# One fixed matmul order for every attention period, and batch 1's second-norm transposes inside the last h1 product

## What is computed

```python
x = x + attn(layernorm(x))     # causal, 16 heads of 64; q, k, v and output projections
x = x + xattn(layernorm(x))    # one head of 256 onto 64 context rows per batch, masked by columns
x = x + ffn(layernorm(x))      # w3 gelu(h2 gelu(h1 (silu(w1 x) * (w2 x)))), ternary weights, scaled
```

## Time and profile before

| | |
|---|---|
| median of 3 runs | 1447.77 us (1446.35 to 1448.05) |
| profiled execution | 1446.44 us, of which the span from the first to the last instruction is 1444.7 us |
| mean granted TensorE clock over the span | 0.997 |
| busy share of the span | PE 99%, PEld 85%, DVE 84%, ACT 70%, POOL 42% |
| the chain that ended last | PE 90%, DVE 5%, ACT 3%, issue 1%, POOL 1% |
| DMA | 113.54 MB, mean 79 GB/s |

### The profile page before, as it was taken

One profiled execution on the slowest core, in us unless ns is written; L12 is line 12 of the kernel. 1 busy time (PEld: TensorE's weight loads), 2 busy tenths in 40 slices (PEclk: granted clock), 3 DMA queues, 4 the chain that ended last, 5 costly groups with the idle time before them and its releaser, 6 DMA issues.

```text
span 1444.7 us, 29203 instructions
## 1 busy us (share of the span) xinstructions
PE 1424.8 (99%) x10408; PEld 1230.6 (85%) x10408; DVE 1210.4 (84%) x3004; ACT 1010.2 (70%) x2382; POOL 603.2 (42%) x883
## 2 busy tenths in 40 slices
...
GB/s 162 2 1 2 60 1 38 24 2 59 2 16 45 2 60 1 2 60 2 16 74 74 186 154 146 197 159 126 146 136 99 209 316 118 31 147 60 118 54 36
DMA packets 78277, 113.54 MB, mean 79 GB/s; under 512 B 4768, under 2 KB 54304, under 8 KB 77216
## 3 DMA queue, kind: packets, MB, share of 16 engines
...
## 4 chain that ended last, share of the span: by engine, by line
PE 90%; DVE 5%; ACT 3%; issue 1%; POOL 1%; DMA 0%; DVEq 0%
PE bank L1606 14%; PE bank L957 10%; PE bank L929 8%; PE bank L877 8%; PE bank L1433 8%; PE bank L878 7%; PE bank L879 7%; PE bank L1435 7%; PE bank L941 5%; PE bank L1624 4%; PE bank L1560 2%; PE bank L1551 2%; PE bank L1553 2%; PE bank L1549 2%; ACT P L1011 1%; PE bank L1443 1%
## 5 line engine op out<-in xcount | busy, mean ns | idle before, releaser
L1011 ACT ACTIVATE P<-P,stats 128x256 f32<-128x256 f32 (+3 forms) x512 | 289.8, 574 | 105.5 <-DVE stats L1113 104.1
L1143 POOL TENSOR_SCALAR P<-P,stats 128x512 f32<-128x512 f32 (+3 forms) x512 | 269.0, 543 | 111.4 <-DVE stats L1121 109.3
L1113 DVE CUSTOM_DVE_ANT_0 P<-bank,cmask 128x256 f32<-128x256 f32 (+3 forms) x512 | 217.0, 486 | 1.5 <-PE bank L929 0.4
L1027 DVE TENSOR_TENSOR PT<-bank,PT 128x512 fp32r<-128x512 f32 (+1 forms) x384 | 206.6, 592 | 5.6 <-ACT PT L980 4.6
L1606 PE MATMUL bank<-op,ws 128*128 128x512 f32 x896 | 205.9, 390 | 0.0
L1433 PE MATMUL bank<-Hb,hw 128*128 128x512 f32 x512 | 202.3, 395 | 0.8 <-DVE Hb L1809 0.8
L1606 PEld LDWEIGHTS bank<-op,ws 128*128 128x128 f32 x896 | 167.4, 188 | 34.0
L957 PEld LDWEIGHTS bank<-PT,V 128*128 128x128 f32 x1024 | 162.3, 190 | 19.1 <-DVE PT L1027 3.9
L980 ACT ACTIVATE PT<-bank 128x512 fp32r<-128x512 f32 (+1 forms) x384 | 173.0, 528 | 5.8 <-PE bank L941 5.6
L1435 PE MATMUL bank<-Hb,hw 128*128 128x512 f32 x448 | 175.5, 392 | 0.0
L957 PE MATMUL bank<-PT,V 128*128 128x512 f32 (+3 forms) x1024 | 171.7, 320 | 2.9 <-DVE PT L1027 2.9
...
## 6 DMA issues: line engine op xcount, KB each, us to landing
...
```

The source lines that it names most:

```text
L1011: e.activation(p, p, ACT.Exp, bias=st_[:, k:k + 1], scale=-1.0, accum_out=st_[:, 8 + k:9 + k]).then_inc(s_exp, 1)
L1027: return e.tensor_tensor(dst, a, b.bitcast(f32), ALU.subtract)
L1113: e.tensor_tensor_reduce(P_tile(P, i, a), banks["S", P, S_ITEM[i]][a][:, slice(*S_COLS[i])], cmask[:, 512 - n:512], -1.0, 3.0e38, ALU.add, ...
L1143: e.tensor_scalar(p, p, stats[P % 4][:, k:k + 1], 1.0, ALU.mult, ALU.mult).then_inc(s_norm, 1)
```

## The change

The lists in `ATTENTION` are rewritten for PE, ACT, DVE and POOL; each holds the same steps as before, and SP's list and everything that `later()` makes are unchanged. From the period of `S.7` to that of `S.60` TensorE's sequence is now the same throughout: S.P.3 S.P.2 S.P.1, T.P-1 in the order 2, 0, 1, k.P+1, v.P+3, q.P+1, AV.P-1.0, AV.P-1.1, O.P-2. Most periods had it before; in the others `v` stood ahead of `k` or behind `q`, a T stood between two S, or two T were exchanged. The first seven and the last three periods are in new orders of their own, and `idle.1` moves to the front. The other engines' lists follow. Lines of the lists that the text speaks of, old and new (PE, then ACT, then DVE):

```diff
-        idle.0 rows.0.0 rows.0.1 idle.1 k.0 q.0 v.0 S.0.3 S.0.2 S.0.1 k.1 q.1 v.1 v.2 v.3 S.1.3 S.1.2 T.0.0
-        S.1.1 T.0.2 T.0.1 k.2 q.2 v.4 AV.0.0 AV.0.1 S.2.3 S.2.2 T.1.0 S.2.1 T.1.2 T.1.1 v.5 k.3 q.3 AV.1.0
...
+        idle.1 idle.0 rows.0.0 rows.0.1 k.0 q.0 v.0 S.0.3 S.0.2 S.0.1 k.1 q.1 v.1 S.1.3 S.1.2 S.1.1 v.2 v.3
+        T.0.0 T.0.2 k.2 T.0.1 q.2 v.4 AV.0.0 AV.0.1 S.2.3 S.2.2 T.1.0 T.1.1 S.2.1 T.1.2 k.3 q.3 v.5 AV.1.0
...
-        k.12 v.14 q.12 AV.10.0 AV.10.1 O.9 S.12.3 S.12.2 S.12.1 T.11.2 T.11.0 T.11.1 v.15 k.13 q.13 AV.11.0
-        AV.11.1 O.10 S.13.3 S.13.2 S.13.1 T.12.2 T.12.0 T.12.1 k.14 q.14 v.16 AV.12.0 AV.12.1 O.11 S.14.3
-        S.14.2 S.14.1 T.13.2 T.13.1 T.13.0 O.12 v.17 k.15 q.15 AV.13.0 AV.13.1 S.15.3 S.15.2 S.15.1 T.14.2
-        T.14.0 T.14.1 v.18 k.16 q.16 AV.14.0 AV.14.1 O.13 S.16.3 S.16.2 S.16.1 T.15.2 T.15.0 T.15.1 k.17 v.19
+        k.12 v.14 q.12 AV.10.0 AV.10.1 O.9 S.12.3 S.12.2 S.12.1 T.11.2 T.11.0 T.11.1 k.13 v.15 q.13 AV.11.0
+        AV.11.1 O.10 S.13.3 S.13.2 S.13.1 T.12.2 T.12.0 T.12.1 k.14 v.16 q.14 AV.12.0 AV.12.1 O.11 S.14.3
+        S.14.2 S.14.1 T.13.2 T.13.0 T.13.1 k.15 v.17 q.15 AV.13.0 AV.13.1 O.12 S.15.3 S.15.2 S.15.1 T.14.2
+        T.14.0 T.14.1 k.16 v.18 q.16 AV.14.0 AV.14.1 O.13 S.16.3 S.16.2 S.16.1 T.15.2 T.15.0 T.15.1 k.17 v.19
...
-        S.37.3 S.37.2 S.37.1 T.36.2 T.36.0 T.36.1 k.38 q.38 v.40 AV.36.0 AV.36.1 O.35 S.38.3 S.38.2 S.38.1
...
+        S.37.3 S.37.2 S.37.1 T.36.2 T.36.0 T.36.1 k.38 v.40 q.38 AV.36.0 AV.36.1 O.35 S.38.3 S.38.2 S.38.1
...
-        S.61.2 S.61.1 k.62 T.60.0 T.60.1 q.62 xt.0.0.0 xt.0.0.1 O.59 AV.60.0 AV.60.1 S.62.3 S.62.2 k.63 T.61.0
-        T.61.2 O.60 q.63 S.62.1 T.61.1 xk.0 xk.1 S.63.3 S.63.2 AV.61.0 AV.61.1 T.62.2 xv.0 xv.1 xf.0 xf.1
-        T.62.0 T.62.1 S.63.1 xc xs.0 AV.62.0 AV.62.1 O.61 xpt.0 T.63.0 T.63.1 T.63.2 xo.0.0 xo.0.1 O.62
-        AV.63.0 xv.2 AV.63.1 xv.3 xt.0.1.0 xt.0.1.1 O.63 ft.2 g.0.0 u.0.0 g.0.1 O.64 u.0.1 g.0.2 u.0.2 g.0.3
-        u.0.3 g.0.4 u.0.4 g.0.5 u.0.5 g.0.6 u.0.6 g.0.7 ft.3 u.0.7""",
+        S.61.2 S.61.1 k.62 T.60.0 T.60.1 xt.0.0.0 xt.0.0.1 q.62 AV.60.0 AV.60.1 T.61.2 O.59 S.62.3 S.62.2
+        S.62.1 T.61.0 k.63 q.63 O.60 T.61.1 xk.0 xk.1 S.63.3 S.63.2 AV.61.0 AV.61.1 xv.0 xv.1 xf.0 xf.1 T.62.2
+        T.62.0 xs.0 S.63.1 T.62.1 xc AV.62.0 AV.62.1 T.63.2 O.61 T.63.0 xpt.0 T.63.1 xo.0.0 xo.0.1 AV.63.0
+        AV.63.1 xv.2 xv.3 O.62 xt.0.1.0 xt.0.1.1 ft.2 O.63 O.64 g.0.0 u.0.0 g.0.1 u.0.1 g.0.2 u.0.2 g.0.3
+        u.0.3 g.0.4 u.0.4 g.0.5 u.0.5 g.0.6 u.0.6 ft.3 g.0.7 u.0.7""",
...
-        wh.0 rows_high.0.0 rows_high.0.1 wh.1 wh.2 wh.3 wh.4 kh.0 qh.0 wh.5 wh.6 vc.0 wh.7 e.0.3.1 e.0.2.0
...
-        fh.6 xfh.0 e.63.2.1 xfh.1 ph.62.0.1 e.63.2.0 ph.62.1.1 big.5 xcc ph.62.0.0 e.63.0.1 e.63.0.0 e.63.1.1
-        ph.62.1.0 xvh.0 xvh.1 e.63.1.0 fh.7 xe.0 yo.62.0 yo.62.1 xph.0 big.6 ph.63.0.0 ph.63.1.1 ph.63.2.0
-        ph.63.2.1 ph.63.0.1 ph.63.1.0 fh.8 big.7 yo.63.0 yo.63.1 big.8 xth.0.1.0 xth.0.1.1 fh.9 fh.10 fh.11
...
+        e.63.2.0 bqh e.63.2.1 big.5 ph.62.0.0 ph.62.1.1 ph.62.1.0 e.63.0.0 xcc xvh.0 xvh.1 e.63.1.0 e.63.1.1
+        e.63.0.1 yo.62.0 yo.62.1 fh.7 xe.0 ph.63.0.0 ph.63.2.1 ph.63.0.1 big.6 ph.63.2.0 xph.0 ph.63.1.1
+        ph.63.1.0 fh.8 big.7 big.8 yo.63.0 yo.63.1 fh.9 fh.10 fh.11 xth.0.1.0 xth.0.1.1 big.9 silu.0.0
...
-        ls0a ls.0 lc.0 ln0.0 ln2.0 rows_low.0.0 rows_low.0.1 wl.0 wl.1 wl.2 wl.3 wl.4 kl.0 ql.0 wl.5 m.0.3.1
...
+        ls0a ls.0 lc.0 ln0.0 ln2.0 wl.0 wl.1 rows_low.0.0 rows_low.0.1 wl.2 wl.3 wl.4 kl.0 ql.0 wl.5 m.0.3.0
...
-        m.15.1.0 m.15.0.1 pl.14.0.0 pl.14.2.0 m.15.1.1 pl.14.0.1 r.15.2 pl.14.2.1 pl.14.1.0 pl.14.1.1 ln2.3
...
+        m.15.0.1 m.15.2.1 m.15.1.0 pl.14.2.1 pl.14.0.0 pl.14.2.0 ln2.3 pl.14.0.1 r.15.2 pl.14.1.1 pl.14.1.0
...
-        m.37.3.1 m.37.2.0 m.37.0.0 m.37.1.1 m.37.0.1 m.37.1.0 m.37.2.1 pl.36.2.0 pl.36.0.1 pl.36.0.0 lc.6
...
+        m.37.0.0 m.37.2.1 m.37.1.0 m.37.0.1 m.37.1.1 pl.36.0.0 pl.36.2.0 lc.6 pl.36.0.1 pl.36.2.1 pl.36.1.0
```

The second part of the change moves the transposes of `xt.1.1` from their place ahead of `h.0.7` into that product, behind its piece c = 4:

```diff
-        def hidden(out, src, m, ready, new=None, scores_of=0):
+        def transpose_rows(b, which, j):
+            out, = claim(w, ("xt", b, which, j))
+            if (b, which, j) == (0, 1, 0):
+                keep_warm(e, out, 22)
+            w.wait_ge(s_ln2, ln_at(b, which) + 4)
+            for t in range(NT):
+                i = e.transpose(out[:, t * 128:t * 128 + 128], xns[:, t, j * 128:j * 128 + 128], ident[:, :])
+            i.then_inc(s_x2T, 1)
+
+        def hidden(out, src, m, ready, new=None, scores_of=0, rows_of=0):
             for c in range(8):
                 if c == 4 and scores_of:
                     scores_by_rows(scores_of)
                 if c == 5 and new == 0:
                     transpose_flag(0)
+                if c == 5 and rows_of:
+                    for j in range(2):
+                        transpose_rows(rows_of, 1, j)
                 hidden_step(out, src, m, ready, c)
             return hidden_end(out, src, m, new)
...
             elif kind == "xt":
-                b, which, j = a
-                out, = claim(w, item)
-                if a == [0, 1, 0]:
-                    keep_warm(e, out, 22)
-                w.wait_ge(s_ln2, ln_at(b, which) + 4)
-                for t in range(NT):
-                    i = e.transpose(out[:, t * 128:t * 128 + 128], xns[:, t, j * 128:j * 128 + 128], ident[:, :])
-                i.then_inc(s_x2T, 1)
+                if a[:2] != [1, 1]:
+                    transpose_rows(*a)
...
@@ -1581,7 +1587,8 @@
                     hidden_end(out, src, 1).then_inc(s_hid, 1)
                 else:
                     hidden(out, src, m, ready, 0 if (b, m) == (0, 3) else None,
-                           b + 1 if m == (3 if b == 0 else 1) and b + 1 < B else 0).then_inc(s_hid, 1)
+                           b + 1 if m == (3 if b == 0 else 1) and b + 1 < B else 0,
+                           1 if (b, m) == (0, 7) else 0).then_inc(s_hid, 1)
```

More of the change, by code:

```diff
@@ new lines @@
+    "DVE": """
+        ls0a ls.0 lc.0 ln0.0 ln2.0 wl.0 wl.1 rows_low.0.0 rows_low.0.1 wl.2 wl.3 wl.4 kl.0 ql.0 wl.5 m.0.3.0
+        m.0.2.0 m.0.3.1 m.0.2.1 m.0.0.0 m.0.0.1 m.0.1.0 wl.6 kl.1 ql.1 r.0.2 wl.7 m.0.1.1 m.1.3.1 m.1.3.0
+        m.1.0.1 m.1.0.0 r.0.0 wl.8 m.1.2.1 m.1.2.0 m.1.1.0 wl.9 m.1.1.1 pl.0.2.1 pl.0.2.0 pl.0.0.1 pl.0.0.0
+        ls.1 pl.0.1.1 pl.0.1.0 r.1.2 r.1.0 lc.1 kl.2 ql.2 ys.0.0 ys.0.1 m.2.3.1 m.2.3.0 m.2.0.0 m.2.2.0
+        m.2.2.1 m.2.1.1 pl.1.0.0 m.2.0.1 m.2.1.0 pl.1.1.1 pl.1.1.0 pl.1.2.1 pl.1.0.1 pl.1.2.0 ln0.1 r.2.2
+        ln2.1 kl.3 ql.3 r.2.0 ys.1.0 ys.1.1 m.3.3.1 m.3.3.0 m.3.2.0 m.3.0.0 m.3.2.1 m.3.1.0 m.3.0.1 pl.2.0.0
+        m.3.1.1 pl.2.2.0 pl.2.0.1 pl.2.2.1 pl.2.1.0 pl.2.1.1 ls.2 r.3.2 r.3.0 os.1 kl.4 ql.4 ys.2.0 ys.2.1
+        m.4.3.1 m.4.3.0 m.4.2.0 m.4.0.0 m.4.1.0 m.4.0.1 m.4.1.1 m.4.2.1 pl.3.0.1 pl.3.2.0 pl.3.2.1 pl.3.1.0
+        pl.3.0.0 pl.3.1.1 r.4.2 lc.2 kl.5 ql.5 rows_low.1.0 rows_low.1.1 r.4.0 ys.3.0 ys.3.1 os.2 m.5.3.0
+        m.5.3.1 m.5.0.0 m.5.2.0 m.5.1.0 m.5.1.1 m.5.2.1 m.5.0.1 pl.4.2.0 pl.4.1.1 pl.4.0.0 pl.4.0.1 pl.4.2.1
+        ln0.2 pl.4.1.0 kl.6 ql.6 r.5.2 r.5.0 ys.4.0 ys.4.1 os.3 m.6.3.0 m.6.3.1 m.6.0.0 m.6.2.0 m.6.1.0
+        m.6.0.1 m.6.2.1 m.6.1.1 pl.5.0.1 pl.5.0.0 pl.5.2.0 pl.5.2.1 pl.5.1.1 pl.5.1.0 kl.7 r.6.2 ql.7 ys.5.0
@@ L282 @@
-        pl.46.1.1 ln2.7 kl.48 ql.48 ys.46.0 ys.46.1 r.47.0 os.45 m.48.3.1 m.48.3.0 m.48.2.0 m.48.0.0 m.48.2.1
-        m.48.0.1 m.48.1.0 m.48.1.1 pl.47.0.0 pl.47.0.1 pl.47.2.0 pl.47.2.1 pl.47.1.0 pl.47.1.1 kl.49 r.48.2
+        m.19.3.0 m.19.2.0 m.19.0.0 m.19.2.1 m.19.1.0 m.19.0.1 pl.18.0.0 m.19.1.1 pl.18.2.0 pl.18.0.1 tt2.3.3
+        r.19.2 pl.18.2.1 pl.18.1.1 pl.18.1.0 tt2.3.1 tt2.3.2 tt2.3.0 kl.20 ql.20 ys.18.0 ys.18.1 r.19.0 os.17
+        m.20.3.0 m.20.3.1 m.20.0.0 m.20.2.0 m.20.1.0 m.20.1.1 m.20.0.1 m.20.2.1 pl.19.0.0 pl.19.2.0 pl.19.0.1
@@ new lines @@
+        m.23.0.1 m.23.1.1 ln2.4 pl.22.2.0 pl.22.0.1 r.23.2 pl.22.2.1 pl.22.0.0 pl.22.1.1 pl.22.1.0 kl.24 ql.24
+        ys.22.0 ys.22.1 r.23.0 os.21 m.24.3.1 m.24.3.0 m.24.2.0 m.24.0.0 m.24.1.0 m.24.0.1 m.24.2.1 pl.23.2.0
+        pl.23.0.0 m.24.1.1 pl.23.2.1 pl.23.0.1 r.24.2 pl.23.1.0 pl.23.1.1 kl.25 ql.25 ys.23.0 ys.23.1 r.24.0
+        os.22 m.25.3.0 m.25.3.1 m.25.2.0 m.25.0.0 m.25.2.1 m.25.0.1 m.25.1.0 m.25.1.1 pl.24.0.0 pl.24.0.1
+        pl.24.2.0 pl.24.2.1 pl.24.1.1 pl.24.1.0 kl.26 r.25.2 ql.26 ys.24.0 ys.24.1 r.25.0 os.23 m.26.3.1
@@ new lines @@
+        m.31.1.1 m.31.0.1 pl.30.0.1 pl.30.2.0 pl.30.2.1 pl.30.0.0 pl.30.1.0 kl.32 pl.30.1.1 r.31.2 ln2.5 ql.32
+        ys.30.0 ys.30.1 r.31.0 os.29 m.32.3.0 m.32.3.1 m.32.2.0 m.32.0.0 m.32.1.1 m.32.1.0 m.32.0.1 m.32.2.1
+        pl.31.0.0 pl.31.2.0 pl.31.0.1 pl.31.1.1 pl.31.2.1 pl.31.1.0 r.32.2 kl.33 ql.33 ys.31.0 ys.31.1 r.32.0
+        os.30 m.33.3.0 m.33.3.1 m.33.2.0 m.33.0.0 m.33.2.1 m.33.0.1 m.33.1.0 m.33.1.1 pl.32.0.0 pl.32.0.1
+        pl.32.2.0 pl.32.2.1 pl.32.1.1 pl.32.1.0 kl.34 r.33.2 ql.34 ys.32.0 ys.32.1 r.33.0 os.31 m.34.3.1
```

561 lines of the change are left out of this document (270 added, 291 removed).

## The result

The changed kernel takes 1438.82 us (median; 1437.99 to 1439.29) beside 1447.99 us for the kernel before in the same session: ratio 0.9943, 95% interval 0.9930 to 0.9956. A fifth run of the changed kernel, 5281.41 us at a granted clock of 1.00, is left out of this range and of the ratio. The forecast was 1442.6 us with a range from 1438.0 to 1447.3. Run once more, in another session, the changed kernel took 1439.50 us beside 1446.55, ratio 0.9951 (0.9938 to 0.9965). So the gain is 7 to 9 us; the forecast had 5.2.

The account below looks back on a forecast made before the run. TensorE, busy for 99% of the span, was taken as the bound, its idle in three short places. The terms -3.7 - 1.0 + 0.5 - 1.0 = -5.2 us gave a median of 1442.6 us, range 1438.0 to 1447.3.

Parts of the forecast that it names:

- Transposes into the last product: Batch 1's second-norm transposes, moved into h.0.7: wait saving 2.1 us and half-clock stretch 1.6 us, together -3.7 us.
- The same sequence in every period: Steady attention, 74.38 to 730.78 us: only waits can change; -1.0 us, between -4.0 and +5.1 us.
- The sign that was named: Steady attention: periods of 11.65 us throughout would show the forecast right.
- The start: First periods, idle.1 moved to the very front: +0.5 us net, between -0.6 and +4.6 us.
- The step on `k.0`: Start: with the fillers in front, k.0 starts near 12.5 us, +0.9 us.
- Its terms, 5.6, 2.6 and 1.4 us: Start: small fillers until 5.6 us, 24 full transposes 2.6, 40 small ones 1.4; rows start near 9.9 us.
- something comes back: First periods: VectorE work runs ahead of the rows' split, so +0.9 us on k.0 becomes +0.5 us net.
- End of attention: End of attention, same work in another order on TensorE, ScalarE, VectorE: -1.0 us, between -4.4 and +3.7 us.
- D: End of attention loses both waits: -4.4 in place of -1.0, so -8.6 us, 1439.2 us; chance 0.11.
- A: Steady periods: the fixed sequence waits, 0.27 us a period, +11 us there, +7 in all, 1455 us; chance 0.07.
- B: Start at half clock: small transposes do not raise it, k.0 at 16.1 us, +4.6 us, 1446.7 us; chance 0.11.
- C: Waits only change place, at batch 1's transposes or end of attention: about -0.6 us, 1447.2 us; chance 0.12.

Follow-up runs that it names:

- pos7: The changed kernel with batch 1's transposes ahead of the last piece of h.0.7 (c == 7) instead of the sixth: 0.49 us longer behind the end of h.0.6.
- start: The kernel before with the changed lists of all engines up to P = 9 alone, idle.1 in front: ratio 0.9987 (0.9978 to 0.9997).
- steady: The kernel before with the changed lists between P = 9 and P = 58 alone: ratio 0.9991 (0.9982 to 1.0001).
- fill_end: The changed kernel with transposes of the identity put into its three holes at the end of attention: ratio 0.9957 (0.9942 to 0.9972).

## Why the prediction was right, and where its terms were off

*Transposes into the last product*, forecast -3.7: measured alone -3.9. The hole was worth 2.3 us, its whole length, where 0.2 us of waiting had been allowed for; the clock was worth the 1.6 us of the forecast. `g.1.0` waits for nothing, as counted; `pos7` shows that the cover is used up two pieces later.

*The same sequence in every period*, forecast -1.0 from 74 us to 731 us: -1.3 in the trace of after, and 1.2 us by the sorted column. That the new lists bring this gain is shown; that it is waits is shown for a part only. The idle in this stage fell by 0.5 us (656.40 - 655.19 = 1.21 before, 655.08 - 654.35 = 0.73 after). The rest must lie in matmuls that start late by less than their modelled length, and which ones is open. The sign that was named, 11.65 us throughout, did not come: 8 of 56 periods are over 11.8 us. The period at 97 us and the longest one kept their length, and in the six periods with the first `v` of a batch there is no idle of over 0.15 us ahead of `v`.

*The start*, forecast +0.5 to the sixth period: -0.1. The step on `k.0` (+0.9) came out: +1.05 in the trace, 0.92 when `idle.1` goes back. That it came so near is luck, since three errors cancel. Its terms, 5.6, 2.6 and 1.4 us, add to 9.6 for the start of the rows and not to 9.9; the sixty small transposes took 3.4 us in place of 4.1; and the 24 full ones took 3.5 in place of 2.6, because the clock rose only at 6.51 us, among them. The rows began at 9.85. The step that failed is the half sentence "something comes back": it was taken at 0.4 us, and the new order of the first periods gives 1.6 us between `k.0` and P = 9 (108.7 for 110.3 us). Of the idle in the first five periods 1.4 us are left of 2.9. The range given there named these 2.9 us, so the room had been seen and mostly left out.

*End of attention*, forecast -1.0 to `u.0.7`: -0.83 alone, -1.10 in the kernel after. It came about in another way than the step says. The wait of 1.57 us and the one of 0.80 us ahead of `AV.63.0` went and the one of 1.19 us shrank to 0.28, but three holes of 1.26, 1.16 and 1.65 us stand in their place, and one stretch at half clock stayed. Not counted at all was a wait that lies behind the stage: `h.0.1` stood 0.77 us for `Hb`, and with the new order it does not. Another -0.99 us to the end of `h.0.6` in the run of the end lists alone.

So of the 7.4 us by which the last matmul moved, 5.2 were in the sum; the rest is 0.2 of the first term, 0.3 of the second, 0.6 of the start and 1.1 of the end with `h.0.1` behind it. The 9.2 us between the medians hold some 2 us more, which is spread between runs: the profiled run of before was 1.5 us under its median in that session, and that of after 0.5 above. The result lies 0.8 us inside the lower end of the range, and that end was set by D, which did not come about as told.

*The rivals.* A did not come: the periods have 0.7 us of idle in all, and none has more than 0.4. B did not: the clock rose at 6.51 us, and in `start` at 5.01, when sixty small transposes and one full one were all that had been issued; `k.0` came at 12.61 us and not at 16.1. The Trainium skill's sentence that the upper level does not engage for transposes (TensorE: Matmul & The Clock Gate, Part 4: PE-mode transpose) doesn't hold in any of these runs: in all of them the clock rose between 5.01 and 7.43 us, ahead of the first matmul with data. C is true in small: at the end of attention waits change place, as `steady` and `fill_end` show, but not at the transposes. D's time (1439.2) is near the result, its reason isn't: the two waits that it counts went or shrank, but others came in their place.
